# Scan to residual through DRAM for both halves, halved statistics, and a projection that takes its high halves first

## What is computed

```python
h = nan_to_num(embed_table[ids])                       # (64, 256, 256)
x = layernorm(h)
log_f, log_i = log_sigmoid(x @ Wf.T), log_sigmoid(x @ Wi.T)
log_c = log_g(x @ Wh.T)
# a scan over the 256 tokens of each sequence, from 0.5:
# s[t] = sigmoid(f)[t] * s[t-1] + sigmoid(i)[t] * g(c)[t]
h = h + s
x = layernorm(h)
u = bitlinear(x, w_fc) + gate * (x @ v.T @ fast_b.T @ u.T)   # hidden 1024, rank 16
h = h + bitlinear(relu(u) ** 2, w_proj)
```

## Time and profile before

| | |
|---|---|
| median of 3 runs | 913.5 us (913.47 to 913.63) |
| the profiled execution's own time | 913.92 us |
| span of its trace | 912.1 us |
| busy time of PE, DVE, ACT, POOL | 880.3, 755.8, 788.5, 418.5 us |
| granted TensorE clock, mean | 0.998 of full speed |

### The profile page before, as it was taken

The page is one execution under the profiler, slowest core; times in us unless marked ns, Lnnn a source line. Parts: engine busy times, 40 slices in busy tenths (PEclk is TensorE's granted clock), DMA queues, the critical chain, the costliest instruction groups (busy, mean ns, idle before and its releaser), DMA issues.

```text
span 912.1 us, 18335 instructions
## 1 busy us (share of the span) xinstructions
PE 880.3 (97%) x5505; PEld 482.1 (53%) x5505; DVE 755.8 (83%) x1338; ACT 788.5 (86%) x1195; POOL 418.5 (46%) x457
## 2 busy tenths in 40 slices
PE   4979999999999999999999999999999999999997
PEld 2435554555555455555455555545555545555554
DVE  6988888788888888888888888888888888888766
ACT  5677998888998888998888899888889988899884
POOL 7446544445544445554444554444555444433110
PEclk9999999999999999999999999999999999999999
DMA  4123434432333443333443233344333334423311
GB/s 146 24 53 68 92 73 87 99 78 69 89 82 75 98 98 61 79 85 74 91 98 78 68 88 82 75 97 98 63 81 89 73 85 97 97 51 82 78 47 47
DMA packets 225372, 72.88 MB, mean 80 GB/s; under 512 B 200134, under 2 KB 220176, under 8 KB 225344
## 3 DMA queue, kind: packets, MB, share of 16 engines
q1 hardware_dynamic: 219200, 68.33, 33.8%
q0 software_dynamic: 6144, 4.21, 2.0%
HBM read 27.68 MB, written 24.64 MB: 57 GB/s over the span
## 4 chain that ended last, share of the span: by engine, by line
PE 85%; DVE 4%; ACT 4%; issue 2%; DMA 2%; SPq 1%; POOL 1%; ACTq 0%; POOLq 0%; DVEq 0%
PE bank L848 33%; PE bank L870 22%; PE y_ps L784 22%; PE bank L884 3%; PE turned L824 1%; ACT sq L584 1%; PE turned L761 1%; ACT normed L509 1%; ACT relu L571 1%; SPq L338 1%; DMA x_cols<-x_rows 1%; PE turned L772 1%; PE turned L771 1%; DMA spill<-hid_blocks 1%; DVE hid L1277 0%
## 5 line engine op out<-in xcount | busy, mean ns | idle before, releaser
L870 PE MATMUL bank<-x_cols,fc_t 128*128 128x512 f16 x1024 | 244.1, 381 | 3.6 <-ACT relu L571 3.6
L420 POOL TENSOR_SCALAR var_eps<-moments 128x4 f32<-128x4 f32 x64 | 59.5, 929 | 387.9 <-DVE moments L1020 387.6
L848 PE MATMUL bank<-x_cols,w_hi 128*128 128x512 f16 x768 | 229.8, 381 | 4.9 <-ACT forget L560 2.0
L848 PE MATMUL bank<-x_cols,w_lo 128*128 128x512 f16 x768 | 229.4, 380 | 0.0
L784 PE MATMUL y_ps<-proj_t,sq_hi 128*128 128x256 bf16 x1024 | 225.6, 273 | 3.0 <-DVE sq_lo L1203 3.0
L784 PE MATMUL y_ps<-proj_t,sq_lo 128*128 128x256 bf16 x1024 | 225.6, 273 | 0.0
L571 ACT ACTIVATE relu<-bank,relu_scale 128x512 f32<-128x512 f32 x256 | 159.3, 689 | 39.6 <-PE bank L884 39.0
L410 POOL DMA_INDIRECT rows_raw<-table,idx_now x128 | 148.0, 1156 | 59.9 <-issue 30.8
L870 PEld LDWEIGHTS bank<-x_cols,fc_t 128*128 128x128 bf16 x1024 | 95.0, 98 | 130.8 <-issue 28.3
L1203 DVE TENSOR_TENSOR sq_lo<-sq,sq_hi 128x1024 f16<-128x1024 f32 x128 | 150.6, 1214 | 5.8 <-ACT sq L584 5.7
L509 ACT ACTIVATE normed<-h,shift,rstd 128x256 f32<-128x256 f32 x256 | 132.7, 601 | 5.4 <-POOL shift L428 5.4
(11 more groups left out here) (143 smaller groups left out, 919.7 us busy)
## 6 DMA issues: line engine op xcount, KB each, us to landing
out<-out_sb SPq DMA_DIRECT2D x31, 512.0 KB, 3.0
spill<-hid_blocks SPq DMA_DIRECT2D x30, 256.0 KB, 2.1
hid_rows<-spill SPq DMA_DIRECT2D x120, 64.0 KB
rows_raw<-table,idx_now POOLq DMA_INDIRECT x128, 2.6
x_cols<-x_rows SPq DMA_TRANSPOSE x120, 3.6
sq<-w_fc SPq DMA_DIRECT2D x1, 1024.0 KB, 5.5
pj_raw<-w_proj SPq DMA_DIRECT2D x1, 1024.0 KB, 4.8
out<-out_sb SPq DMA_DIRECT2D x2, 256.0 KB, 2.1
```

Of the source, the lines that this page charges most:

```text
L848: ins = pe.matmul(gate_bank(p, par)[:, :], w[:, k, q, :], x_part(0, par, part)[:, :, k, :], start=(k == 0 and w is w_hi and part == 0), st ...
L870: ins = pe.matmul(fc_bank(f, par)[:, :], fc_t[:, f, k, :], x_part(1, 0, part)[:, :, k, :], start=(opens and k == 0 and part == 0), stop=(n ...
```

## The change

1. **The upper half takes the lower half's way.** `hid_blocks`, `hid_rows` and `spill` get a second half each; `turn_blocks(e)`, `spill_blocks(n, e)` and `fetch_rows(n, e)` run for both. `turn_upper` is left in step N − 1 = 31 alone. The block transpose writes its blocks in another order, so that `fetch_rows` reads runs of 128 elements, not of 32. On SP the upper half's write and reads stand behind `turn_rows(0, n+1)`, then a wait for the reads' landing, then `store(n-2)`.
2. **DVE's order.** `residual` is split: the lower half's sum and statistics, then half of the guard's sum, `square_low(n-1, 0)` and `(n-1, 1)` (before at the head of the next step), then the upper half's sum and statistics, the aggregation, the other half of the guard's sum, and the statistics of chunk n + 2 (before `measure_next` of the next step).
3. **Statistics of the second norm** are of 128 elements, eight a chunk; variance plus epsilon and minus the mean move from POOL to DVE (`sum_up`).
4. **ACT** takes `cand_sig` and `cand_lin` of the lower half ahead of `normalise(1, m)`. In the last chunk the high square of pair 3 is ACT's.
5. **The projection** takes all high halves, then all low halves.
6. `w_raw` (start-up only) becomes a part of `relu`'s buffer.

```diff
@@ -323,20 +325,19 @@
                 sp.wait_ge(pj_ready, k + 1)
                 sp.dma_start_transpose(proj_t[:, :, k * P:(k + 1) * P], pj_c[:, k, :]).then_inc(pj_landed, 16)
-            def spill_blocks(c):
-                sp.wait_ge(blocks_ready, c - 1)
+            def spill_blocks(c, e):
+                sp.wait_ge(blocks_ready[e], c - 1)
                 pass_on(sp, sp_passed, c)
-                sp.dma_start(spill[:, :], hid_blocks[:, :]).then_inc(blocks_spilled, 16)
-            def fetch_rows(c, par):
-                sp.wait_ge(blocks_spilled, 16 * (c - 1))
+                sp.dma_start(spill[e, :, :], hid_blocks[:, e, :]).then_inc(blocks_spilled[e], 16)
+            def fetch_rows(c, e):
+                sp.wait_ge(blocks_spilled[e], 16 * (c - 1))
                 pass_on(sp, sp_passed, c)
-                rows = spill.rearrange("(i t) (j q c) -> i t j q c", t=BLOCK, j=TILES, q=B)
+                rows = spill[e, :, :].rearrange("(i t) (q x) -> i q t x", t=BLOCK, q=B)
                 for i in range(B):
-                    sp.dma_start(hid_rows[:, :, BLOCK * i:BLOCK * (i + 1)],
-                                 rows[i].rearrange("t j q c -> q t j c")).then_inc(blocks_moved[par], 16)
+                    sp.dma_start(hid_rows[:, e, i * P:(i + 1) * P], rows[i]).then_inc(blocks_moved[e], 16)
             def store(c, par):
                 first = sp.snap(c * CHUNK) if not isinstance(c, int) else c * CHUNK
...
@@ -367,12 +368,16 @@
                     pass_on(sp, sp_passed, n)
                     turn_rows(1, n - 1, 0)
                 if known_below(n, N):
-                    spill_blocks(n)
-                    fetch_rows(n, par)
+                    spill_blocks(n, 0)
+                    fetch_rows(n, 0)
                 if known_below(n, N - 1):
                     wait(sp, gate_done, 6 * n)
                     pass_on(sp, sp_passed, n)
                     turn_rows(0, n + 1, 1 - par)
+                    spill_blocks(n, 1)
+                    fetch_rows(n, 1)
+                    sp.wait_ge(blocks_moved[1], 16 * B * (n - 1))
+                    pass_on(sp, sp_passed, n)
                 store(n - 2, par)
             steps(sp, step)
...
@@ -414,14 +419,17 @@
             def root(k, c):
-                pool.wait_ge(moments_ready[k], TILES * (c + 1))
                 wait(pool, normed_ready[k], TILES * c)
-                pass_on(pool, pool_passed, c)
-                pool.tensor_scalar(var_eps[k][:, :], moments[k][:, :, 1], EPS, None, ALU.add)\
-                    .then_inc(var_ready[k], 1)
-                pool.tensor_scalar(minus_mean[k][:, :], moments[k][:, :, 0], -1.0, None, ALU.mult)\
-                    .then_inc(var_ready[k], 1)
+                if k == 0:
+                    pool.wait_ge(moments_ready[k], TILES * (c + 1))
+                    pass_on(pool, pool_passed, c)
+                    pool.tensor_scalar(var_eps[k][:, :], moments[k][:, :, 1], EPS, None, ALU.add)\
+                        .then_inc(var_ready[k], 1)
+                    pool.tensor_scalar(minus_mean[k][:, :], moments[k][:, :, 0], -1.0, None, ALU.mult)\
+                        .then_inc(var_ready[k], 1)
                 pool.wait_ge(var_ready[k], 2 * c + 2)
+                if k == 1:
+                    pass_on(pool, pool_passed, c)
                 pool.tensor_tensor(rstd[k][:, :], var_eps[k][:, :], minus_half[:, :], ALU.pow)\
                     .then_inc(rstd_set[k], 1)
                 pool.wait_ge(rstd_set[k], c + 1)
...
                     low_high(1)
                     back(2)
                     return
+                if front:
+                    evict(n, par, 0, 2, cand_sig, ACT.Sigmoid)
+                    evict(n, par, 0, 3, cand_lin, ACT.Identity, 0.5)
                 normalise(1, m, h1[:, 1 - par, :, :])
                 if front:
                     x_high(1, m)
                 else:
                     cols_high(1, 1)
                 if front:
-                    evict_low()
+                    evict(n, par, 0, 1, inp, ACT.Sigmoid)
+                    evict(n, par, 0, 0, forget, ACT.Sigmoid)
                     if ahead:
                         normalise(0, n + 1, h0[:, 1 - par, :, :])
                         x_high(0, n + 1)
...
@@ -778,33 +793,35 @@
                     pe.wait_ge(pj_landed, 16 * KD)
                     pe.wait_ge(u_ready, 2)
-                def tile(f, j):
-                    for part in (sq_hi, sq_lo):
-                        ins = pe.matmul(y_ps[:, j, :], part[:, f, j * P:(j + 1) * P], proj_t[:, f, :],
-                                        start=(f == 0 and j % 2 == 0 and part is sq_hi),
-                                        stop=(f == FC - 1 and part is sq_lo), skip_group_check=True)
+                def tiles(part, p, rows):
+                    for f in (2 * p, 2 * p + 1):
+                        for j in rows:
+                            ins = pe.matmul(y_ps[:, j, :], part[:, f, j * P:(j + 1) * P], proj_t[:, f, :],
+                                            start=(f == 0 and j % 2 == 0 and part is sq_hi),
+                                            stop=(f == FC - 1 and part is sq_lo), skip_group_check=True)
                     return ins
...
+                if isinstance(c, int) and c == N - 1:
+                    for p in range(4):
+                        if p < 3:
+                            pe.wait_ge(sq_hi_ready, 4 * c + p + 1)
+                        else:
+                            pe.wait_ge(sq_hi_last, 1)
+                        tiles(sq_hi, p, range(TILES))
+                        pe.wait_ge(sq_lo_ready, 4 * c + p + 1)
+                        if p < 3:
+                            tiles(sq_lo, p, range(TILES))
+                    for b in range(2):
+                        tiles(sq_lo, 3, (2 * b, 2 * b + 1)).then_inc(y_done, 1)
                     return
-                for b in range(2):
-                    for f in (FC - 2, FC - 1):
-                        for j in (2 * b, 2 * b + 1):
-                            ins = tile(f, j)
-                    ins.then_inc(y_done, 1)
+                for part, ready in ((sq_hi, sq_hi_ready), (sq_lo, sq_lo_ready)):
+                    for p in range(4):
+                        if isinstance(c, int) and c == N - 2 and part is sq_lo and p == 2:
+                            turn_normed(1, N - 1)
+                        pe.wait_ge(ready, 4 * c + p + 1)
+                        ins = tiles(part, p, range(TILES))
+                ins.then_inc(y_done, 1)
...
@@ -936,7 +953,7 @@
                         pe.wait_ge(u_landed, 16)
                     narrow(0, 4)
                 wide(4, True)
-                if front and not first:
+                if isinstance(n, int) and n == N - 1:
                     turn_upper(n)
                 wide(5, True)
...
+            def measure_half(c, rows, e):
+                for j in range(TILES):
+                    dve.bn_stats(stats[1][:, j, e, :], rows[:, j, e * P:(e + 1) * P]).then_inc(stats_ready[1], 1)
+            def sum_up(c):
+                dve.wait_ge(stats_ready[1], TILES * KD * (c + 1))
+                wait(dve, var_ready[1], 2 * c)
+                pass_on(dve, dve_passed, c)
+                for j in range(TILES):
+                    dve.bn_aggr(moments[1][:, j, :], stats[1][:, j, :, :].rearrange("p e s -> p (e s)"))\
+                        .then_inc(moments_ready[1], 1)
+                dve.wait_ge(moments_ready[1], TILES * (c + 1))
+                wait(dve, rstd_ready[1], c)
+                dve.tensor_scalar(var_eps[1][:, :], moments[1][:, :, 1], EPS, None, ALU.add).then_inc(var_ready[1], 1)
+                dve.tensor_scalar(minus_mean[1][:, :], moments[1][:, :, 0], -1.0, None, ALU.mult).then_inc(var_ready[1], 1)
             def x_low(k, c):
...
@@ -1277,28 +1323,46 @@
                         dve.tensor_tensor_scan(hid[:, e, at], forget[:, e, at], value[:, e, at], 0.5,
                                                ALU.mult, ALU.add).then_inc(scanned, 1)
-                def turn_blocks():
-                    dve.wait_ge(scanned, 4 * n + 2)
-                    wait(dve, blocks_spilled, 16 * (n - 2))
-                    dve.transpose(hid_blocks[:, :], hid[:, 0, :]).then_inc(blocks_ready, 1)
-                def residual(c, at):
-                    if late:
-                        dve.wait_ge(blocks_moved[par], 16 * B * h)
-                        dve.wait_ge(out_ready, c - 1)
-                        dve.tensor_tensor(h1[:, at, :, 0:P], hid_rows[:, :, :], h0[:, at, :, 0:P], ALU.add)\
-                            .then_inc(h1_low, 1)
-                        dve.wait_ge(hid_turned, c + 1)
-                        dve.tensor_tensor(h1[:, at, :, P:D], turned_half, h0[:, at, :, P:D], ALU.add)\
-                            .then_inc(h1_ready, 1)
-                        dve.wait_ge(h1_low, c - 1)
+                def turn_blocks(e):
+                    dve.wait_ge(scanned, 4 * n + 2 * e + 2)
```

(47 more changed lines are left out.)

73 lines of the change are left out of this document (37 added, 36 removed).

## The result

The changed kernel takes **988.4 us** (median of 4 runs, 987.8 to 989.7) against 913.5 us (4 runs, 913.4 to 913.6) of the kernel before: 1.081 times as long, 95% interval 1.080 to 1.083. Forecast were 904.0 us, with a range to 918. The profiled execution took 987.8 us, its span 985.9.

What follows compares the result with a forecast made beforehand. PE was taken to set the pace at 26.89 us a step; 29 × (0.44 − 0.15) = 8.4 plus 1.1 at the end came off 913.9, giving 904.4, and the median 0.4 lower, 904.0 us; range 899.5 to 918.

Steps and rivals of the forecast that it cites:

- the part on SP and DRAM: Upper half's write and reads through DRAM: written from 23.5, last read issued at 27.0, rows landing 29.1, before 29.5.
- SP is free at 22.7, before the 23.5: SP's queue: after the lower reads and two transposes for 2.63, SP is free before the upper blocks' write.
- The mechanism of gain: PE sets the pace; taking upper transposes off it saves 0.44 us a step, 12.8 us over 29 steps.
- case B: Second norm's columns land late for PE's low-rank product; 0.25 to 0.5 us a step given back, 907 to 914; chance 0.22.
- the 4.4 us of waits: PE's waits for the second norm's columns and part_lo, taken as 0.15 us a step over 29 steps.
- case E: SP's reads stay slow to issue, 1.1 us each; upper rows land at 33; 980 us or more; chance 0.04.
- a quarter of the packets: Argument against slow reads on SP: 128 runs of 512 bytes in place of 512 runs of 128 bytes.
- Case C: POOL's power and shift slip behind x_low if DVE ends over 0.4 later; PE waits 1.3 a step; 935; chance 0.14.
- mixtures: Only some steps have the first norm's root miss its slot on POOL; times down to 915, within chance 0.14.
- Case D: POOL's running power keeps DVE's x_low out until 11.65; step of 27.2 us, time 920; chance 0.04.
- the rule of exclusion: Two-input SBUF instruction on DVE and SBUF-reading one on POOL exclude each other; whoever starts first keeps the pair throughout.

Runs made afterwards that it cites:

- experiment 6: Changed kernel with each half's four reads cut to fill 32 partitions with four runs each, not all 128 with one: 902.5 us against 912.3 before.
- Experiment 1: Changed kernel with the upper half of the scan transposed on PE again, rest of the change kept: 913.3 us against 912.4 before.
- experiment 11: experiment 6 with two spare row statistics of 0.35 us each at the end of DVE's step: 922.6 us against 912.9 before.
- experiment 10: experiment 6 with each of the upper half's four reads cut in two, of 31 partitions and 1: 1262.0 us, ratio 1.382 to the kernel before.
- experiment 9: experiment 6 with each of the upper half's four reads cut in two, of 16 and 16 partitions: 940.6 us, ratio 1.030 to the kernel before.
- experiment 7: experiment 6 with the lower half's reads cut as in the changed kernel, only the upper half by 32 rows: 921.8 us, ratio 1.010 to before.
- experiment 5: Changed kernel with the upper half read back by one straight transfer of 2048-byte rows, leaving its order wrong: 914.3 us against 912.3 before.

## Why the prediction was wrong

**The step that failed** stands in the part on SP and DRAM: "The last read is issued at 27.0 and should land 2.1 later (a write's round trip), 29.1." The row behind it was a write whose pattern runs over 128 partitions; the reads' pattern is outermost 4. Measured 3.98 us instead of 2.1. The slack of the whole design at this point was 0.4 us (29.1 against 29.5), so 1.9 more could not be hidden: DVE waits 1.9 to 3.7 us a step, at the head of a queue on which the second norm, two low squares and the next first norm depend.

The other terms of that part were small errors, to the same side: reads issued in 0.55 apiece, not 0.45; the write landing 2.5 later, not 2.2 (from the write's issue to the rows' landing 8.24 us, 361.56 to 369.80, instead of 5.6, and 1.9 of the difference is the last landing); and SP free at 361.44, over 1 us after the blocks were turned (by 360.22), since the transposes took 3.76 for 2.63. That last term is the prediction's "SP is free at 22.7, before the 23.5" and comes of the same reads. The size fits, too: 29 waits of 2.8 us are 82 us, an estimate, and the forecast was 84 us too low.

**The evidence was in the trace of before**, in its step 2, and was not weighed. Its reads have the outermost extent 4, too. SP's last read there and the residual that waits for it, from the chain and from DVE in order of time:

```profile
91.19 1.38 SPq L338
92.68 1.79 SPq L305
```
```profile
95.21 0.69 DVE L1291 TENSOR_TENSOR h<-hid_rows,h 128x512 f32<-128x512 f32 x1 [0.32 <-DMA hid_rows<-spill]
```

Issued at 91.19, used at 95.21: 4.0 us (with runs of 128 bytes, so the row alone did not say what makes it slow, but it spoke against 2.1). In the steady part the lower residual had time to spare, so no row there shows it; a row of the start does.

**The mechanism of gain was right**, and experiment 6 measures it: 902.5 us for 904.0. Step by step, with the time from the first gate product (336.20 in that trace):

| | predicted | experiment 6 |
|---|---|---|
| power of the first norm | 10.5 | 10.47 |
| x_low | 10.91 | 10.91 |
| low-rank product wants x_cols | 15.55 | 15.71 |
| upper half written | 23.5 | 23.36 |
| last read's issue begins | 27.0 | 26.84 |
| upper residual | 29.5 | 29.34 |
| step | 26.60 | 26.46 |

The statistics of halves took 0.87 us for four, as forecast, the two small sums 0.17 and 0.16, the strided transpose 0.71 as before. The landing of the second norm's columns (case B) cost nothing, where 0.15 a step was put in. So the total agrees more closely than its terms do: steps of 26.46 for 26.89 and 0.6 at the end make some 13 us, and 9.8 came (912.3 to 902.5). The start takes back 0.9 (the first write to DRAM at 86.48 instead of 85.60); the other 2 us are not accounted for. That these losses come near the 4.4 us of waits which the prediction put in for another reason is luck. Experiment 1 shows the same from the other side: without PE's relief (0.44 a step) nothing is gained, and nothing lost.

**The rivals.** What came was nearest to *case E* (chance 0.04, "980 or more", "about 30 us a step"): its effect in full, including the second normalisation 3 us late, but by another way. It had the reads slow to issue; they were quick to issue (0.55) and slow to land. So the rival had the right place and the wrong quantity, and the argument against it ("a quarter of the packets") spoke to the issue alone. *Case C* is real in its order of events (experiment 11 shows it in rows): 0.4 us was predicted to be enough to bring it about, 0.7 did in every second step; for 922.6 the prediction's "mixtures" stand, not its 935, and PE's wait is 0.94 us in those steps, not 1.3 in each. In the change it comes on top (the wait of 1.68 at 380.12). *Case D* fell: in experiment 6 the power runs from 346.67 for 1.04 us and x_low starts at 347.11 and takes 1.22.

```profile
346.67 1.04 POOL L434 TENSOR_TENSOR rstd<-var_eps,minus_half 128x4 f32<-128x4 f32 x1
```
```profile
347.11 1.22 DVE L1068 TENSOR_TENSOR x_rows<-normed,x_rows 128x1024 f16<-128x1024 f32 x1 [0.61 <-ACT x_rows L525]
```

Here the row, and not the rule of exclusion quoted beside the case, decides for DVE as the later one.

**What is behind the extent.** The runs show: extent 4 lands in 4.0 us, 32 in some 2.2, 31 holds up even the issues, at equal bytes and runs. The Trainium skill (DMA: Bandwidth & Descriptors, "Why a DMA increments its semaphore by 16 and not by 1") gives a rule that fits: a transfer is spread over the largest number of DMA engines up to 16 that divides the outermost extent greater than 1 of both patterns. By it 32 and 16 have 16 engines, 4 has four, 31 has one. The traces agree, and in more than the times. Here are the stretches in which the upper half's reads move their 256 KB, in the change, in experiment 6 and in experiment 10 (columns as in the earlier trace rows; the last but one is the busy share of the core's 16 DMA engines):

```profile
365.50:369.30 3.80, 3.80 (x22) 1.98 (x21) 0.80 (x1) 3.80 (x6) 0.00 (x0) 1.00 0.23 68
```
```profile
362.70:364.70 2.00, 2.00 (x11) 0.90 (x10) 2.00 (x3) 2.00 (x3) 0.00 (x0) 1.00 0.46 130
```
```profile
369.80:383.50 13.70, 10.48 (x73) 6.84 (x70) 3.00 (x4) 7.74 (x10) 0.00 (x0) 0.97 0.07 19
```

Rate times length is some 260 KB in each, so nothing else runs there. 0.23 of 16 engines are 3.7, 0.07 are 1.1, and in experiment 6 it is 7.4 for about half as long: the same bytes, with four, one and more engines at work.

The pages count packets, too, those of SP's queue at the same 83.5 MB:

| | packets | against experiment 6 |
|---|---|---|
| experiment 6 | 195440 | |
| the change | 192608 | 12 fewer for each of 236 reads |
| experiment 9 (16 + 16) | 197296 | 64 more for each of 29 sets of upper reads |
| experiment 10 (31 + 1) | 194164 | 44 fewer for each of 29 sets |

One small packet at the end of a read for each engine in it gives just these numbers: 16 a read and 64 a set in experiment 6, 4 a read in the change, 8 × 16 = 128 a set in experiment 9, and 4 × (1 + 4) = 20 in experiment 10, where the read of a single partition has its four runs as the extent. No row names a DMA engine, so this is a reading of shares and counts, but nothing measured here speaks against it. Left open is why the transposes behind such reads take SP 4.1 us at times (308.60 in experiment 7) and 2.4 at others (360.87 in experiment 5).

## What to carry to other kernels

Of a transfer that somebody waits for, read the outermost extent of both patterns and not only bytes and runs: a view that splits a dimension for gathering (4 × 32 rows) can put a small number in front, and the same data by 32 rows cost 86 us less of 988. Before a step goes behind a round trip through DRAM, take the landing from a row of the same pattern (look at the start and the end of the trace, where cover is thin), and compare its error with the slack. When a wait is predicted to be covered by 0.4 us in an in-order queue, forecast the time for the case that it is not: here it decided between −10 and +75 us.

## What the hardware showed that was not expected

- Four reads of 64 KB with extent 4: issued in 2.21 us, last landing 3.98 behind its issue. With extent 32: 1.73 us and, by the store behind it, no more than 2.2. With 31 + 1 partitions eight issues take 11.38 us, and 3.58 with 16 + 16. While such reads run, the core's 16 DMA engines are busy for 0.23 (extent 4), 0.46 (32) and 0.07 (31 + 1).
- The transposes between two such sets of reads take SP 3.76 us instead of 2.55: a slow transfer is paid by the queue behind it, too.
- POOL's power on 128x4 takes 1.04 us where it starts ahead of x_low with nothing else running on DVE (346.67 in experiment 6), and 1.87 to 2.09 where x_low or a low square already runs (353.07 in experiment 11; 346.86 and 377.35 in the change); x_low takes 1.2 in either case.
